# Output written back by two issuing engines instead of one: four image transfers move from SyncE to ScalarE

## The reference

```
patches = _patchify(x)                                # (8, 64, 1024)
tok     = einsum('bld,td->blt', patches, w) + b       # (8, 64, 192)
h       = concat(cls_tok, tok)                        # (8, 65, 192)
layer 0: h += attention0(layernorm(h));  h += moe0(layernorm(h))   # 8 experts of width 768, the best 2 used
layer 1: h += attention1(layernorm(h));  h += moe1(layernorm(h))   # quantised attention, 12 heads; 16 experts, the best 8 used
return h                                              # (8, 65, 192), float32
```

## Time and profile before

| what | value |
|---|---|
| median of three runs | 339.03 us (337.79 to 339.14) |
| the profiled execution, its own time | 338.6 us |
| its span, first to last instruction | 336.7 us |
| busy in the span | PE 292.5, DVE 263.4, ACT 209.1, POOL 13.7 us |
| first output DMA issued | 329.80 us |
| output DMAs | 8 of 48 KB, 1 of 6 KB |

### The profile page before, as it was taken

One profiled execution on the slowest core, in us unless ns is written; L12 is line 12 of the kernel. 1 busy time (PEld: TensorE's weight loads), 2 busy tenths in 40 slices (PEclk: granted clock), 3 DMA queues, 4 the chain that ended last, 5 costly groups with the idle time before them and its releaser, 6 DMA issues.

```text
span 336.7 us, 6345 instructions
## 1 busy us (share of the span) xinstructions
PE 292.5 (87%) x2385; PEld 265.4 (79%) x2385; DVE 263.4 (78%) x780; ACT 209.1 (62%) x519; POOL 13.7 (4%) x38
## 2 busy tenths in 40 slices
PE   8999999999999999999878126299678999999991
PEld 7979669999999999999867014188455789999981
DVE  0356758999998989898777898989777679999851
ACT  1064377777686677777659397885123778778750
POOL 0520000000000000000010003200000000000000
PEclk9999999999999999999999655589989999999996
DMA  7991302143250504110000000004100035543402
GB/s 240 317 285 23 145 3 97 34 163 119 79 196 2 197 0 166 37 73 2 0 1 3 0 0 2 0 2 142 77 2 0 2 101 173 173 146 94 94 3 48
DMA packets 10542, 27.29 MB, mean 81 GB/s; under 512 B 1352, under 2 KB 2184, under 8 KB 10512
## 3 DMA queue, kind: packets, MB, share of 16 engines
q1 hardware_dynamic: 10096, 26.20, 23.8%
q0 software_dynamic: 416, 0.68, 0.7%
HBM read 26.43 MB, written 0.45 MB: 80 GB/s over the span
## 4 chain that ended last, share of the span: by engine, by line
DVE 42%; PE 34%; ACT 16%; issue 5%; DMA 1%; DVEq 0%; ACTq 0%
PE bank L622 11%; ACT hid_hi L1078 7%; DVE hid_lo L1417 7%; DVE hidden_area L1412 5%; DVE fc_lo L1391 5%; PE bank L602 5%; PE bank L732 4%; DVE pj_parts L1394 3%; PE bank L691 3%; ACT pj_parts L1056 3%; PE bank L592 2%; PE bank L674 2%; PE bank L672 2%; DVE bn L1310 1%; DVE score_area L1702 1%
## 5 line engine op out<-in xcount | busy, mean ns | idle before, releaser
L1078 ACT ACTIVATE hid_hi<-hidden_area 128x260 fp32r<-128x260 f32 x144 | 55.6, 422 | 39.3 <-DVE hidden_area L1412 38.3
L622 PE MATMUL bank<-hid_hi,pj_parts 128*128 128x260 f32 x288 | 77.2, 289 | 0.3
L1417 DVE TENSOR_TENSOR hid_lo<-hidden_area,hid_hi 128x260 fp32r<-128x260 f32 x144 | 56.3, 427 | 10.3 <-ACT hid_hi L1078 1.5
L622 PEld LDWEIGHTS bank<-hid_hi,pj_parts 128*128 128x128 f32 x288 | 54.1, 188 | 2.9 <-DVE hid_lo L1417 1.8
L1071 ACT ACTIVATE hidden_area<-bank 128x260 f32<-128x260 f32 x144 | 48.0, 375 | 4.1 <-PE bank L674 3.8
L592 PE MATMUL bank<-zeros 128*128 128x260 bf16 x249 | 36.5, 301 | 8.2 <-ACT hidden_area L1221 6.4
L622 PE MATMUL bank<-xt_hi,fc_hi 128*128 128x260 f32 x144 | 41.2, 286 | 1.1 <-ACT hidden_area L1071 0.8
L674 PE MATMUL bank<-xt_lo,fc_lo 128*128 128x260 f32 x144 | 41.3, 287 | 0.0
L691 PE MATMUL bank<-hid_hi,pj_parts 128*128 128x260 f32 x144 | 40.8, 283 | 0.0
L672 PE MATMUL bank<-xt_lo,fc_hi 128*128 128x260 f32 x144 | 40.7, 283 | 0.0
L622 PE MATMUL bank<-xt_lo,fc_hi 128*128 128x260 f32 x144 | 40.7, 282 | 0.0
(11 more groups left out here) (294 smaller groups left out, 557.3 us busy)
## 6 DMA issues: line engine op xcount, KB each, us to landing
raw_area<-fc_dram SPq DMA_DIRECT2D x8, 768.0 KB, 4.6
raw_area<-pj_dram SPq DMA_DIRECT2D x8, 576.0 KB, 6.1
xn<-comb_dram SPq DMA_DIRECT2D x12, 260.0 KB, 4.1
raw_area<-fc_dram SPq DMA_DIRECT2D x6, 512.0 KB, 4.1
embed_area<-embed_in_dram SPq DMA_DIRECT2D x8, 352.0 KB, 6.3
hidden_area<-comb_dram SPq DMA_DIRECT2D x9, 260.0 KB, 4.3
raw_area<-pj_dram SPq DMA_DIRECT2D x6, 384.0 KB, 4.5
score_area<-w_l_dram SPq DMA_DIRECT2D x1, 576.0 KB, 9.3
```

The source lines that it names most:

```text
L622: mm = pe.matmul(out, lhs[a], rhs[b], start=start and n == 0, stop=stop and n == 2, skip_group_check=True)
L1078: act.activation(hid_hi[:, x % 3, tok], hid_w[:, x % 2, tok], ACT.Copy).then_inc(hid_hi_ready[y], 1)
L1417: dve.tensor_tensor(hid_lo[:, x % 3, tok], hid_w[:, x % 2, tok], hid_hi[:, x % 3, tok].bitcast(F32), ALU.subtract).then_inc(hid_lo_ready[y ...
```

## The change

Four of the eight image transfers are issued by ScalarE, at the end of its stream, and count on a semaphore of their own. SyncE keeps the images 0, 1, 4 and 5 and the class tokens; ScalarE gets 2, 3, 6 and 7. Every image transfer now has its own wait for `h_done`, where before only the first and the fifth had one. SyncE's last wait is for both semaphores. The transfers themselves, their sources, destinations and sizes, are the same.

```diff
+        out_done_act = sem("out_done_act")
...
+        def patches_out(queue, b, done):
+
+            lo = (b % 2) * PATCH
+            queue.dma_start(t["out"][b, 1:S, :], h[lo:lo + PATCH, b // 2, :]).then_inc(done, 16)
...
         def _(sp):
...
-            for b in range(B):
-                lo = (b % 2) * PATCH
-                if b % 4 == 0:
-
-                    sp.wait_ge(h_done, 4 + b // 4)
-                sp.dma_start(t["out"][b, 1:S, :], h[lo:lo + PATCH, b // 2, :]).then_inc(out_done, 16)
+            for b in (0, 1, 4, 5):
+                sp.wait_ge(h_done, 4 + b // 4)
+                patches_out(sp, b, out_done)
             sp.wait_ge(h_done, 6)
             sp.dma_start(t["out"][:, 0, :], h[0:B, 4, :]).then_inc(out_done, 16)
-            sp.wait_ge(out_done, 16 * (B + 1))
+            sp.wait_ge(out_done, 16 * 5)
+            sp.wait_ge(out_done_act, 16 * 4)
...
         def _(act):
...
             ffn(1)
             sums_out(1)
+            for b in (2, 3, 6, 7):
+                act.wait_ge(h_done, 4 + b // 4)
+                patches_out(act, b, out_done_act)
```

## The result

| | before | after |
|---|---|---|
| median | 339.08 us (337.79 to 339.22, 4 runs) | 336.77 us (336.37 to 337.08, 4 runs) |
| profiled execution: time, span | 338.6, 336.7 us | 336.37, 334.3 us |
| first output issue to the end of the span ("the tail") | 6.9 us | 4.7 us |
| time outside the span | 1.9 us | 2.07 us |

The ratio is 0.9945, 95% interval 0.9929 to 0.9961: shorter by 2.3 us or 0.55%. The forecast was 336.5 us, a gain of 2.3. Two repeats beside the kernel before gained 2.08 and 1.90 us (experiments 8 and 4).

What follows compares the result with a forecast made beforehand. Nine output issues in a row on SyncE were taken to bound the tail. Terms of -2.54, +0.03 and +0.2 us gave -2.3: 336.3 from the profiled execution, 336.7 from the median, forecast 336.5 us, range 335.3 to 338.9.

Steps and rivals of the forecast that it cites:

- SyncE's five transfers, 2.54 us: On SyncE's output issues: five instead of nine, four steps of 0.635 us fewer, saving 2.54 us.
- The waits in front of each image, 0: On SyncE's stream: two more waits, both already satisfied when reached, costing 0 us.
- ScalarE's step p = 0.635: On ScalarE's four image issues: each step takes 0.635 us, as on SyncE.
- The landing, 1.0 us after SyncE's last issue: At SyncE's last wait: the class tokens land 1.0 us after their issue ends, as before.
- two bursts at once, 0.2: On the 16 DMA engines: if the last bursts of both issuing engines meet, the later lands 0.2 us late (bounds 0 to 0.2).
- No backlog builds up: On the DMA engines: two bursts together fill only some 0.64 of a step, so nothing queues up.
- The second leg, 0.03 behind the first: At the end: ScalarE's images land by 333.84 us, 0.03 after SyncE is through at 333.81.
- The sum: Over the output tail: -2.54 + 0.03 + 0.2 = -2.3 us, giving a span of 334.4 us.
- rival 1: On both issuing engines: whole issues take turns, records about 1.2 us, no gain, 338.6 to 339.0 us; chance 0.12.
- rival 2: On both issuing engines: 0.4 us of each issue is exclusive, records 0.8 to 0.9, gain 1.6 us; chance 0.15.
- rival 3: On ScalarE: issues cost over 1.47 us a step, so the kernel gets slower; chance 0.08, of over 0.5% 0.05.
- rival 4: Outside the span: a second issuing engine's queue costs 1 us, time 337.3 to 337.7 us; chance 0.07.

Runs made afterwards that it cites:

- experiment 8: The change itself timed again, against the kernel before: 336.67 us against 338.75.
- experiment 4: Two-image transfers on SyncE and ScalarE, against the kernel before: 336.28 us, second time 335.99; the change repeated beside it: 336.98 against 338.88.
- experiment 2: Against the changed kernel, ScalarE issues only images 3 and 7, SyncE the rest: 337.21 us against 338.37 for the kernel before.
- experiment 1: Against the changed kernel, all nine output transfers issued by ScalarE: 338.38 us against 338.37 for the kernel before.
- experiment 3: Against the kernel before, SyncE alone issues five transfers, four of two images each and the class tokens: 336.61 us against 338.75.
- experiment 6: Against the changed kernel, the class tokens move from SyncE to ScalarE: 336.94 us against 338.75 for the kernel before.
- experiment 7's first kernel: Against the changed kernel, all eight image transfers write only 32 of their 64 rows: 335.63 us against 338.88 for the kernel before.
- experiment 5, second kernel: Against the kernel before, two-image transfers spread over SyncE, ScalarE and GpSimd: 335.87 us against 338.75.

## Why the prediction was right

*What bounds the tail.* Right. Issues in a row on one engine were the bound: experiment 2 moves two and gets two steps, experiment 1 moves all and gets nothing, experiment 3 removes four without any other engine and gets as much as the change.

*SyncE's five transfers, 2.54 us.* 332.14 - 329.60 = 2.54.

*The waits in front of each image, 0.* SyncE's steps are 0.60, 0.64, 0.65, 0.65, with a wait at each.

*ScalarE's step p = 0.635.* Alone it is 0.64 (experiment 1). Beside SyncE the three steps are 0.60, 0.91 and 0.65, in the mean 0.72, so its fourth image starts 2.16 us after its first and not 1.90.

*The landing, 1.0 us after SyncE's last issue, and two bursts at once, 0.2.* The place was right and the mechanism only in part. The class tokens landed 1.77 us after their issue and not 1.44: 0.32 us late, where I had 0.2 for a shared share of the engines' work. But the DMA engines weren't full (0.64); the bursts of the two engines follow one another, and the class tokens' burst meets that of ScalarE's last image. "No backlog builds up" was wrong: two bursts of 0.34 us more than fill a step of 0.64, ScalarE's first burst is already held back by 0.27, and its second issue is 0.25 longer.

*The second leg, 0.03 behind the first.* I had ScalarE's transfers down last. By the semaphores they are down at 333.79, 0.12 ahead of the class tokens: three steps took 2.16 instead of 1.90, and the last landing 2.01 instead of the 2.13 that I had as its upper bound.

*The sum.* -2.54 + 0.32 = -2.2, and the tail went from 6.9 to 4.7. It was to be 334.4 - 329.8 = 4.6; the span of 334.3 owes 0.2 to a first issue that came at 329.60 and not at 329.80. The 0.2 us outside the span are a term that the sum did not have. The forecast median of 336.5 stands against 336.77; the median of before moved to 339.08, and the difference of the medians is 2.31. That it meets the forecast gain of 2.3 to the hundredth is luck: 2.2 us from the tail less 0.2 to 0.3 outside it make 1.9 to 2.0, and the repeats gave 2.08 and 1.90, still inside the forecast's 1.7 to 2.54.

*The rivals.* Taking turns for whole issues (rival 1) would have made records of 1.2 us; there are none. A partly exclusive issue (rival 2) was to show as records of 0.8 to 0.9; one of eight is 0.86. Its picture of bursts that follow one another is what the trace shows, only with 0.27 to 0.36 us from one to the next and not 0.4. Two of those are about one step of 0.64, so with two engines it costs some 0.3 us and not 0.9 (2.54 - 1.6); the forecast won over this rival by the size of the burst, not because the bursts were free of each other. Dear issues on ScalarE (rival 3) are refuted by experiment 1. Of rival 4 the size was 1 us; 0.2 is there, and its cause, a second issuing engine, is refuted by the table above.

## What to carry to other kernels

Where a program ends in several small output transfers, look at the issues and not at the bytes: if the DMA engines idle between bursts, the tail is the number of issues on the busiest engine times one step (0.64 us here) and the landing of the last, and it shrinks by spreading them over engines that are already idle or, as well and on one engine alone, by putting more rows behind each partition into one transfer. Do both until the DMA share of the bursts comes near 1 (0.95 here); a third engine brought nothing more here. Don't take the landing of the last transfer as fixed: it grew from 1.44 to 1.77 us with two engines and to 2.2 with larger transfers. Read such a gain from the tail of a profile as well, since the work ahead of it scatters from run to run by more than half the gain.

## What the runs showed that I had not expected

- The length of an issue depends on the partitions of the transfer (0.42 us for 32, 0.60 for 64) much more than on the rows behind each partition (0.64 for 64 partitions of two rows).
- The class tokens' issue takes 0.49 us behind a 64-partition transfer on SyncE, but 0.72 and 0.73 on ScalarE (experiments 1 and 6), and 0.33 on SyncE behind 32-partition transfers, by the row of experiment 7's first kernel:

```profile
331.10 0.33 SPq L531 DMA_DIRECT2D out_dram<-h  x1
```

- On SyncE it is also shorter, 0.39 us, where it starts 0.15 us behind the end of the record ahead of it (experiment 5, second kernel). So the record of an issue contains something of the transfer ahead of it. What, no run here tells.
